# A four-layer graph network in which only the order lists of the five engines change

## The chip, the cores and the metric

The kernel runs on one core of one Trainium2 chip. The metric is device time in microseconds (us) from launch to end. Five engines work side by side, each through its own stream of instructions, in order: TensorE (PE, matmuls and transposes into PSUM), VectorE (DVE), ScalarE (ACT), GpSimd (POOL), and SyncE (SP), which here issues every DMA. They meet at semaphores only.

## The reference, cut to what matters

64 graphs of 256 nodes with 256 features pass through four layers. Each layer is `x = layernorm(x + layer(x))`, with one adjacency mask for all:

```python
# layer 0: e = leaky_relu((x W1)(x W2)^T), masked softmax, relu(att @ (x W3))
# layer 1: h = x W; e = leaky_relu(h a1 + (h a2)^T), masked softmax, elu(att @ h)
# layer 2: out = relu(x mlp1 + b1); unmasked graph attention (512 wide), elu, + residual;
#          relu(. mlp2 + b2); masked graph attention (256 wide), elu, + residual, relu
# layer 3: q, k, v = x wq^T + bq, ...; 4 heads of 64; masked softmax(q k^T / 8) @ v; @ wo^T + bo
```

The 64 graphs don't depend on one another. Matmuls of layers 0 to 2 and of the projections are made three times, on high and low parts of both operands (`hi*lo`, `lo*hi`, `hi*hi`).

## The kernel before, in words

One graph is one sample `t`. Everything of a sample is cut into steps, each on one engine: a few instructions with the semaphores that they wait for. The names say what a step belongs to. PE has `g0 h0 s0 t0 a0 x0` (layer 0: two products, scores, transposes of the probabilities, attention product, transposes of the normalised result), `h1 f1 t1 a1 x1` (layer 1), `m2 n2 c2 r2 f2 d2 b2 v2 w2` (layer 2, first part), `m3 n3 h3 f3 t3 a3 o3 x3` (second part), `q4 k4 v4 s40 s42 a4 y4` (layer 3). The same name on ACT, DVE or POOL is mostly the step that takes that product out of PSUM: ACT rounds to the high part, DVE (or POOL) computes the low part. On DVE `e0 e1 e3` mask the scores, `st`, `ag` take the moments of a layernorm, `n4` applies the last one; on POOL `v0 v1 v3 v4` make its factor, `n0 n1 n3` apply it, and `a0` adds the residual to layer 0's result.

The kernel is a software pipeline, and its order is written out in `ORDERS` (line 9 of kernel.py on): one string for each engine, in which `name:stage` means that in round `k` this engine runs this step for sample `k - stage`. `run` unrolls such a string over 64 samples plus the highest stage. Rounds have no barrier. What is set by a string is the sequence on one engine; rotating a string, with the stages raised by one behind the cut, gives the same sequence.

Layer 3's attention runs through DRAM. For heads 0 and 1 (half 0) and heads 2 and 3 (half 1) PE makes scores (`s40`, `s42`, line 436). DVE masks them (`s40` to `s43`, line 935). ACT takes the exponential (`p40` to `p43`, line 671), DVE a reciprocal (line 944), and POOL multiplies (`d4x`, `p4x`, lines 1060 and 1067). DVE transposes blocks of 32 (`x40`, `x42`, line 950). SP writes the half to DRAM (`o40`, `o42`, line 200, 512 KB) and, once that has landed, reads it back turned (`i40`, `i42`, line 208, four DMAs of 128 KB each). Then PE's `a4` (line 456) multiplies with v: eight matmuls of half 0, a wait, eight of half 1.

SP also loads the sample twice, turned (`lt`, line 186, into `x0T`, which waits until POOL's `l0` of the sample before has read it) and straight (`lx`, line 190, into `x0`, which waits for POOL's `a0` of the sample before), and stores the result (`st`, line 194). `x0T`, `x0` and `p4T` have one buffer each.

Banks 2 and 3 of PSUM are lent in turn to `x3 h3 x0 x1 o3 h1`: each of these PE steps (by `enter`) waits until the one before it has been read out; `h1` so waits for DVE's `r3` (line 898).

Of the kernel before, what the change touches and what calls it, by code (L numbers as in the profile page):

```python
# [5 lines left out]


ORDERS = {
    "sp": "lt:0 o40:7 st:9 o42:7 lx:1 i40:7 i42:7",
    "pe": "h3:8 a0:3 v4:9 f3:8 x0:5 g0:2 s40:9 d2:7 x1:6 t3:8 s42:9 v2:7 a3:8 m2:6 h0:2 b2:7 n2:6 o3:8 w2:7 s0:2 h1:5 c2:6 f1:5 t0:2 a4:9 r2:6 t1:5 x3:8 y4:9 m3:7 n3:7 a1:5 f2:6 q4:8 k4:8",  # L10
    "ac": "t0:3 r2:7 x3:9 m3:8 o3:8 a1:6 f2:7 q4:9 k4:9 h3:8 w2:7 x2:7 a0:3 u3:8 x0:5 p3:8 g0:2 p40:9 t3:8 x1:6 p41:9 p42:9 a3:8 p43:9 m2:6 b3:8 b2:7 h0:2 n2:6 o2:6 s0:2 h1:5 y2:7 p0:2 c2:6 k2:7 u1:5 a4:9 p1:5 z2:7 l0:1 t1:5",
    "dv": "e0:1 st3:7 h1:4 st0:2 n2:6 ag3:7 ag0:2 c2:5 i2:6 e1:4 j2:6 a4:8 z2:6 x3:7 i1:4 t1:4 i0:1 ag4:9 y4:8 r2:5 t0:1 f2:5 st4:8 b1:4 a1:4 b2:5 q4:7 st1:4 ag1:4 h3:6 k4:7 v4:7 e3:6 x0:3 s40:7 s41:7 g0:0 p40:7 t3:6 s42:7 x1:4 p41:7 i3:6 s43:7 p42:7 d2:5 n4:9 c3:6 p43:7 x40:7 b3:6 h0:0 x42:7 a3:6 r3:6 v2:5 z3:6",
    "po": "n1:5 d40:8 p40:8 d41:8 p41:8 d42:8 p42:8 d43:8 p43:8 m2:5 a0:2 v3:7 n3:7 v0:2 l0:0 k4:8 v4:9 m3:6 y1:4 n0:2 v1:4 w2:5",
}


# [1097 lines left out]
```

## Time and profile before

| what | value |
|---|---|
| median of 3 runs | 2921.05 us (2909.83 to 2933.94) |
| the profiled execution | 2918.28 us, its span 2916.5 us |
| PE busy | 2689.4 us, 92% of the span |
| DVE, ACT, POOL busy | 78%, 69%, 53% |
| DMA | 195.17 MB, mean 67 GB/s |
| mean granted TensorE clock | 0.983 |

The profiled execution lies 2.8 us under the median. Its span is counted from the first to the last instruction; 1.8 us lie around it. Busy shares are means over a fill of some 250 us, a long steady part and an end in which stages run out.

### The profile page before, as it was taken

Reading aid. Unit: us, or ns where it says so; the run is one execution under the profiler, and the core shown is the slowest. Engines: PE = TensorE matmul, PEld = TensorE weight load, DVE = VectorE, ACT = ScalarE, POOL = GpSimd, SP = SyncE. Lnnn points to the kernel's source line nnn. Section 1 sums busy time; section 2 is a strip of 40 time slices with the busy share of each in tenths; the row PEclk is TensorE's granted clock in tenths of the full one; section 3 lists DMA queues with packets and bytes.
Section 4 is the critical chain, followed back from the end, with each engine's and each line's share of the span. In section 5 each row is a group of like instructions: output and inputs, shape, how many; then the busy total and the mean of one; then the engine's idle time right before and its main releaser. Section 6 shows DMA issues by size and latency. Waiting matters only on the chain.

```text
span 2916.5 us, 61536 instructions
## 1 busy us (share of the span) xinstructions
PE 2689.4 (92%) x22472; PEld 2551.3 (87%) x22472; DVE 2278.2 (78%) x6124; ACT 1998.7 (69%) x4801; POOL 1556.0 (53%) x2119
## 2 busy tenths in 40 slices
PE   4689999999999999999999999999999999999974
PEld 4589999999999999998999998999999999998863
DVE  3257888888888888888888887888888888888874
ACT  1357777777777776777777777777777777776752
POOL 0235555555555555555556555555655555555542
PEclk9799999999999999999999999999999999999997
DMA  3001222222122122212212221221222122122222
GB/s 109 19 16 37 77 81 64 57 81 80 41 80 81 59 63 80 74 47 81 80 51 71 81 72 49 81 81 48 74 81 70 52 80 80 41 81 73 66 66 73
DMA packets 132766, 195.17 MB, mean 67 GB/s; under 512 B 14832, under 2 KB 97136, under 8 KB 132464
## 3 DMA queue, kind: packets, MB, share of 16 engines
q1 hardware_dynamic: 132464, 191.24, 22.7%
q8 instruction: 178, 2.92, 0.4%
q14 instruction: 124, 1.02, 0.1%
HBM read 107.30 MB, written 83.89 MB: 66 GB/s over the span
## 4 chain that ended last, share of the span: by engine, by line
PE 60%; DMA 13%; ACT 8%; SPq 8%; DVE 6%; issue 4%; POOL 1%; POOLq 0%; DVEq 0%
PE ps L224 29%; DMA p4T<-scratch 10%; PE ps L378 6%; SPq L208 6%; PE ps L240 5%; PE ps L436 4%; PE ps L337 4%; PE ps L233 3%; PE ps L338 3%; DMA scratch<-p 3%; DVE p L950 3%; PE ps L456 2%; ACT p L671 2%; PE ps L360 2%; DVE h_lo L692 1%
## 5 line engine op out<-in xcount | busy, mean ns | idle before, releaser
L1067 POOL TENSOR_TENSOR p<-p,rd 128x512 f32<-128x512 f32 x256 | 269.8, 1054 | 20.0
L671 ACT ACTIVATE p<-p,nmx 128x256 f32<-128x256 f32 x512 | 255.7, 504 | 25.4 <-DVE nmx L935 25.2
L991 POOL TENSOR_TENSOR o1Tp_lo<-o1T,o1Tp_hi 128x1024 fp32r<-128x1024 f32 x64 | 153.8, 2403 | 220.8 <-ACT o1Tp_hi L472 220.8
L1003 POOL TENSOR_SCALAR xn<-act,nmean,rstd 128x256 f32<-128x256 f32 x384 | 243.6, 643 | 18.3 <-POOL rstd L998 11.2
L456 PE MATMUL ps<-p4T,v 128*64 128x256 f32 x1024 | 144.3, 404 | 118.2 <-DMA p4T<-scratch 117.7
L995 POOL TENSOR_TENSOR vare<-mv,eps 128x2 f32<-128x2 f32 x256 | 108.0, 422 | 270.5 <-DVE mv L748 270.5
L1060 POOL TENSOR_TENSOR rd<-some,den 128x2 f32<-128x2 f32 x256 | 53.5, 209 | 354.6 <-DVE den L944 354.6
L456 PEld LDWEIGHTS ps<-p4T,v 128*64 128x64 f32 x1024 | 67.3, 140 | 178.1 <-DMA p4T<-scratch 96.5
L692 DVE TENSOR_TENSOR xnT_lo<-ps,xnT_hi 128x512 fp32r<-128x512 f32 x192 | 132.1, 688 | 114.2 <-ACT xnT_hi L472 114.2
L935 DVE CUSTOM_DVE_ANT_0 p<-ps,mask 128x256 f32<-128x256 f32 x512 | 189.9, 418 | 33.3 <-PE ps L436 33.3
L480 ACT ACTIVATE sco<-sco,nmax 128x256 f32<-128x256 f32 x384 | 191.0, 500 | 28.9 <-DVE nmax L736 28.9
L991 POOL TENSOR_TENSOR x0Tp_lo<-x0T,x0Tp_hi 128x512 fp32r<-128x512 f32 x64 | 112.7, 1761 | 162.4 <-ACT x0Tp_hi L472 162.4
L472 ACT ACTIVATE h_hi<-ps 128x512 fp32r<-128x512 f32 x192 | 114.7, 597 | 112.9 <-PE ps L233 98.6
L998 POOL TENSOR_TENSOR rstd<-vare,mhalf 128x2 f32<-128x2 f32 x256 | 179.7, 702 | 0.0
L736 DVE CUSTOM_DVE_ANT_0 sco<-ps,mask 128x256 f32<-128x256 f32 x384 | 146.4, 417 | 40.0 <-ACT ps L475 40.0
L475 ACT ACTIVATE ps<-ps,cols 128x256 f32<-128x256 f32 x384 | 154.5, 441 | 33.7 <-PE ps L246 33.1
L612 ACT ACTIVATE o3T<-ps,b2m 128x256 f32<-128x256 f32 x128 | 53.8, 471 | 171.3 <-PE ps L378 171.3
L337 PE MATMUL ps<-w_fc_lo,o1Tp_hi 128*128 128x258 f32 x512 | 154.8, 302 | 8.5 <-POOL o1Tp_lo L991 5.9
L692 DVE TENSOR_TENSOR h_lo<-ps,h_hi 128x512 fp32r<-128x512 f32 x192 | 131.1, 683 | 38.4 <-ACT h_hi L472 38.4
L742 DVE BATCH_NORM_STATS2 stat<-act 128x6 f32<-128x256 f32 x384 | 143.4, 414 | 19.9 <-POOL act L1013 14.6
L950 DVE STREAM_TRANSPOSE p<-p 128x1024 f32<-128x1024 f32 x128 | 157.4, 1230 | 0.7 <-POOL p L1067 0.7
L224 PE MATMUL ps<-pfcp_lo,hfc_hi 128*128 128x256 f32 x512 | 155.6, 304 | 2.1 <-ACT rdb L472 2.1
(248 smaller groups left out, 12683.1 us busy)
## 6 DMA issues: line engine op xcount, KB each, us to landing
scratch<-p SPq DMA_DIRECT2D x128, 512.0 KB, 2.9
p4T<-scratch SPq DMA_DIRECT2D x512, 128.0 KB, 3.9
x0T<-in_xT SPq DMA_DIRECT2D x64, 256.0 KB, 4.6
x<-in_x SPq DMA_DIRECT2D x64, 256.0 KB, 3.7
out<-xn SPq DMA_DIRECT2D x64, 256.0 KB, 3.0
o1T<-in_mlp SPq DMA_DIRECT2D x1, 512.0 KB, 4.4
p<-in_mlp SPq DMA_DIRECT2D x1, 512.0 KB, 4.5
att<-in_fc SPq DMA_DIRECT2D x1, 512.0 KB, 5.4
```

The costliest lines, as they stand in the source:

```text
L224: ins = nc.tensor.matmul(dst[:, m, :], lhs[a][:, k, (off + m) * P:(off + m + 1) * P], rhs[b][:, k, :], start=(k == 0 and i == 0), stop=(k ...
L337: nc.tensor.matmul(ps[:, 4, 0:C2], lhs, WP["fc"][b][:, k, 0:C2], start=(k == 0 and i == 0), stop=(k == HT - 1 and i == 2))
L456: ins = nc.tensor.matmul(bank[6][g * HD:(g + 1) * HD, c, :], v4[:, k, h * HD:(h + 1) * HD], p4Tv[:, c, g, k, :, :, :], start=(k == 0), sto ...
L480: ins = nc.scalar.activation(sco[i][:, m, :], sco[i][:, m, :], ACT.Exp, scale=-1.0, bias=nmax[i][:, m:m + 1], accum_out=den[i][:, m:m + 1])
L671: ins = nc.scalar.activation(rows_, rows_, ACT.Exp, scale=-1.0, bias=nmx4[:, h, m:m + 1], accum_out=den4[:, h, m:m + 1])
L692: return V.tensor_tensor(pair[1][:, :, :], whole, pair[0][:, :, :].bitcast(fp32), ALU.subtract)
L935: ins = V.tensor_tensor_reduce(p4v[h // 2][:, h % 2, m, :, :, :].rearrange("p w b j -> p w (b j)"), bank[7 - h % 2][:, m, :].rearrange("p ...
L950: V.transpose(p4[c][:, :, :], p4[c][:, :, :]).then_inc(S["p4x"], 1)
L991: return G.tensor_tensor(lo, whole, hi.bitcast(fp32), ALU.subtract)
L998: G.tensor_tensor(rstd[i][:, :], vare[i][:, :], mhalf[:, :], ALU.pow).then_inc(s_rs, 1)
L1003: ins = G.tensor_scalar(xn[:, m, :], y[:, m, :], nmean[i][:, m:m + 1], rstd[i][:, m:m + 1], ALU.add, ALU.mult)
L1067: G.tensor_tensor(rows_, rows_, rd4[:, h, :].unsqueeze(2).unsqueeze(3).broadcast_to([P, NT, QUADS, CT * QP]), ALU.mult).then_inc(S["p4n"], 1)
```

## The change

Every engine's string is another one. No step, instruction, wait or buffer differs; what differs is the sequence in which each engine comes to them.

```diff
-    "sp": "lt:0 o40:7 st:9 o42:7 lx:1 i40:7 i42:7",
-    "pe": "h3:8 a0:3 v4:9 f3:8 x0:5 g0:2 s40:9 d2:7 x1:6 t3:8 s42:9 v2:7 a3:8 m2:6 h0:2 b2:7 n2:6 o3:8 w2:7 s0:2 h1:5 c2:6 f1:5 t0:2 a4:9 r2:6 t1:5 x3:8 y4:9 m3:7 n3:7 a1:5 f2:6 q4:8 k4:8",
-    "ac": "t0:3 r2:7 x3:9 m3:8 o3:8 a1:6 f2:7 q4:9 k4:9 h3:8 w2:7 x2:7 a0:3 u3:8 x0:5 p3:8 g0:2 p40:9 t3:8 x1:6 p41:9 p42:9 a3:8 p43:9 m2:6 b3:8 b2:7 h0:2 n2:6 o2:6 s0:2 h1:5 y2:7 p0:2 c2:6 k2:7 u1:5 a4:9 p1:5 z2:7 l0:1 t1:5",
-    "dv": "e0:1 st3:7 h1:4 st0:2 n2:6 ag3:7 ag0:2 c2:5 i2:6 e1:4 j2:6 a4:8 z2:6 x3:7 i1:4 t1:4 i0:1 ag4:9 y4:8 r2:5 t0:1 f2:5 st4:8 b1:4 a1:4 b2:5 q4:7 st1:4 ag1:4 h3:6 k4:7 v4:7 e3:6 x0:3 s40:7 s41:7 g0:0 p40:7 t3:6 s42:7 x1:4 p41:7 i3:6 s43:7 p42:7 d2:5 n4:9 c3:6 p43:7 x40:7 b3:6 h0:0 x42:7 a3:6 r3:6 v2:5 z3:6",
-    "po": "n1:5 d40:8 p40:8 d41:8 p41:8 d42:8 p42:8 d43:8 p43:8 m2:5 a0:2 v3:7 n3:7 v0:2 l0:0 k4:8 v4:9 m3:6 y1:4 n0:2 v1:4 w2:5",
+    "sp": "lt:0 i40:8 lx:1 i42:8 o40:7 st:9 o42:7",
+    "pe": "c2:6 f1:5 x3:8 a4:9 r2:6 t1:5 m3:7 n3:7 y4:9 a1:5 f2:6 q4:8 t0:2 h3:7 k4:8 v4:8 f3:7 a0:2 x0:4 s40:8 g0:1 t3:7 s42:8 x1:5 d2:6 a3:7 m2:5 o3:7 b2:6 h0:1 n2:5 v2:6 w2:6 h1:4 s0:1",
+    "ac": "m3:8 o3:8 a1:6 f2:7 q4:9 t0:3 h3:8 w2:7 k4:9 u3:8 x2:7 a0:3 p3:8 x0:5 p40:9 t3:8 p41:9 x1:6 g0:2 p42:9 p43:9 a3:8 m2:6 b2:7 b3:8 h0:2 n2:6 o2:6 y2:7 h1:5 k2:7 c2:6 u1:5 z2:7 s0:2 a4:9 p1:5 x3:8 r2:6 t1:5 p0:2 l0:1",
+    "dv": "r3:7 z3:7 v2:6 st3:7 ag3:7 n2:6 h1:4 i2:6 j2:6 c2:5 e1:4 z2:6 n4:9 st0:2 ag0:2 a4:8 e0:1 x3:7 t1:4 r2:5 y4:8 i1:4 i0:1 f2:5 b1:4 st4:8 a1:4 b2:5 q4:7 t0:1 h3:6 st1:4 ag1:4 k4:7 v4:7 e3:6 s40:7 s41:7 x0:3 p40:7 i3:6 t3:6 s42:7 p41:7 x1:4 s43:7 p42:7 ag4:8 g0:0 d2:5 p43:7 x40:7 c3:6 x42:7 b3:6 h0:0 a3:6",
+    "po": "n0:3 v1:5 n1:5 w2:6 d40:8 p40:8 d41:8 p41:8 d42:8 p42:8 d43:8 p43:8 v4:9 a0:2 m2:5 v3:7 n3:7 v0:2 m3:6 l0:0 y1:4 k4:7",
```

Rotated to one starting point, the strings differ by local moves; the stages change only as the cut goes. On PE, `x1` and `d2` go behind `s42`, `x3` ahead of `a4`, `t0` from ahead of `a4` to behind `q4`, `y4` behind `n3`, `k4` behind `h3`, `a0` behind `f3`, `g0` behind `s40`, and the end of the round is `o3 b2 h0 n2 v2 w2 h1 s0` in place of `h0 b2 n2 o3 w2 s0 h1`. On SP the sequence from `x40` on was `o40 st o42 lx i40 i42 lt`; it becomes `o40 st o42 lt i40 lx i42`, with `lx` for one sample later. On DVE, `n4` leaves its place ahead of `x40`, `b3` and `h0` go behind `x42`, `ag4` comes ahead of `g0`, and `z3` ahead of `v2`. On POOL `v4` and `a0` come directly behind `p43`, ahead of `m2`, `l0` behind `m3`, `n1` ahead of `w2`, and `k4` to the end of the round behind `y1`. On ACT `p43` goes ahead of `a3`, `s0` behind `z2`, `p0` and `l0` to the end behind `t1`, `t0` behind `q4`.

## Rows read from the trace of the kernel before

**Rows 1.** Busy time by engine in the steady part (windows; TensorE's clock, DMA share, GB/s last)

```profile
265.00:2530.00 2265.00, 2182.31 (x18594) 2083.74 (x18593) 1863.76 (x5041) 1653.37 (x3979) 1296.41 (x1751) 1.00 0.24 69
```

**Rows 2.** Waits of PE (total, times, longest): steady part, then its whole span

```profile
PE ps L456 <- DMA p4T<-scratch: 82.3, 82, 1.8
...
PE ps L456 <- DMA p4T<-scratch: 117.7, 92, 12.4
```

**Rows 3.** Timeline of SP: loads of x0T, 55 rounds apart (start, duration)

```profile
256.61 0.43 SPq L186 DMA_DIRECT2D x0T<-in_xT  x1
...
2601.20 0.43 SPq L186 DMA_DIRECT2D x0T<-in_xT  x1
```

**Rows 4.** Timeline of PE around one a4

```profile
1452.72 0.60 PE L240 MATMUL ps<-ident,sco 128*128 128x128 f32 x4
1453.25 1.08 PE L456 MATMUL ps<-p4T,v 128*64 128x256 f32 x8
1455.27 1.08 PE L456 MATMUL ps<-p4T,v 128*64 128x256 f32 x8 [0.93 <-DMA p4T<-scratch]
```

**Rows 5.** Chain of waits, one round, from d2 and s42 to a4's second half

```profile
1434.61 0.98 PE ps L360 x8
...
1436.55 0.91 PE ps L436 x12
...
1445.21 1.16 DVE p L950
...
1450.97 4.26 DMA p4T<-scratch
```

**Rows 6.** Timeline of DVE in the same round: n4, c3, x40, b3, h0, x42, z3

```profile
1440.06 1.07 DVE L972 TENSOR_SCALAR xn<-xn,nmean,rstd 128x256 f32<-128x256 f32 x2
1441.41 0.90 DVE L885 TENSOR_SCALAR act<-act 128x512 f32<-128x512 f32 x1 [0.28 <-ACT act L640]
...
1442.47 1.23 DVE L950 STREAM_TRANSPOSE p<-p 128x1024 f32<-128x1024 f32 x1
1443.73 0.50 DVE L889 TENSOR_SCALAR act<-act 128x512 f32<-128x512 f32 x1
1444.52 0.69 DVE L692 TENSOR_TENSOR h_lo<-ps,h_hi 128x512 fp32r<-128x512 f32 x1 [0.29 <-ACT h_hi L472]
1445.13 1.23 DVE L950 STREAM_TRANSPOSE p<-p 128x1024 f32<-128x1024 f32 x1
...
1448.96 1.04 DVE L902 SCALAR_TENSOR_TENSOR act<-act,xn 128x512 f32<-128x512 f32 x1
```

**Rows 7.** Chain of waits near the end, where SP has no loads left

```profile
2832.22 3.36 DMA scratch<-p
...
2836.89 3.37 DMA p4T<-scratch
```

**Rows 8.** A window of 1 us in the burst of transfers of rows 5

```profile
1454.00:1455.00 1.00, 0.33 (x4) 0.00 (x0) 1.00 (x2) 1.00 (x3) 0.82 (x2) 1.00 1.02 213
```

**Rows 9.** Timeline of PE: first product after transposes

```profile
1418.11 0.37 PE L224 MATMUL ps<-w_woT_lo,qT_hi 128*128 128x256 f32 x1
1418.31 0.28 PE L224 MATMUL ps<-w_woT_hi,qT_lo 128*128 128x256 f32 x1
1418.43 0.28 PE L224 MATMUL ps<-w_woT_hi,qT_hi 128*128 128x256 f32 x1
```

**Rows 10.** One line's instructions, 1000 to 2000 us: ns min/median/max

```profile
L902 DVE SCALAR_TENSOR_TENSOR act<-act,xn x23: 1045/1052/1067, 1020.9 to 1959.9; 128x512 f32<-128x512 f32 x23
...
L806 DVE TENSOR_SCALAR act<-act x23: 408/412/413, 1039.7 to 1979.3; 128x512 f32<-128x512 f32 x23
```

**Rows 11.** Timeline of POOL in the same round: p43, m2, a0

```profile
1442.91 1.04 POOL L1067 TENSOR_TENSOR p<-p,rd 128x512 f32<-128x512 f32 x1
1447.06 2.40 POOL L991 TENSOR_TENSOR o1Tp_lo<-o1T,o1Tp_hi 128x1024 fp32r<-128x1024 f32 x1 [3.11 <-ACT o1Tp_hi L472]
1450.35 1.31 POOL L1013 TENSOR_TENSOR act<-act,x 128x512 f32<-128x512 f32 x1 [0.89 <-DMA x<-in_x]
```

## The prediction, written before the changed kernel was run

> **What bounds the kernel now.** I read the windows first. In the steady part PE is busy for 2182.3 of 2265 us, at full granted clock; DVE has 82%, ACT 73%, POOL 57% [rows 1]. So PE is the bound, and 82.7 us of it are idle. The list of PE's waits for the same stretch has one line: 82.3 us for the landing of `p4T`, in `a4` [rows 2]. The reader is to see that this is the only loss of PE there. The round lasts (2601.20 - 256.61) / 55 = 42.63 us [rows 3], the stretch holds 53.1 of them, and the idle time is 1.55 us a round. The timeline shows where: eight matmuls of half 0 from 1453.25, half 1 only at 1455.27 [rows 4]. Matmuls start 0.12 us apart [rows 9], so half 1 could have started at 1454.21; it is 1.06 us late where the profile calls 0.93 idle. By that ratio the 1.55 us are worth some 1.75 us of round. The round without the wait would be 40.9 us.
>
> The chain of waits says what ends it. PE's `s42` ends at 1437.46, DVE's transpose `x42` at 1446.37, half 1 lands at 1455.23 [rows 5]: 8.9 us over ACT, POOL and DVE, then 8.9 us of transfers. In these the DMA engines are full (share 1.02 at 213 GB/s in the last window but one) [rows 8], so the landing is a matter of bytes queued ahead, not of latency alone.
>
> **The change part by part.** All terms are per round of the profiled execution, 2918.3 us, whose span is 1.8 us less; it lies 2.8 us under the median of the runs, 0.1%, which I neglect.
>
> PE's cover. Between `s42` and `a4` PE gains `x1`, `d2` and `x3` and loses `t0`. Four transposes in a row are 0.53 us to the next step (1452.72 to 1453.25) [rows 4], `d2` is 0.98 [rows 5]. Net +0.53 + 0.98 + 0.53 - 0.53 = 1.5 us; as neighbouring transposes are a little cheaper I take 1.4 (1.2 to 1.5).
>
> The chain from `s42` to `x42`. `n4`, 1.07 us, stood on DVE ahead of `c3` and `x40`; it goes to a place 25 us off. `b3` and `h0` stood between the end of `x40` (1443.70) and `x42` (1445.13), 1.43 us with their waits [rows 6]; they go behind. What is late next: `x42` needs POOL's `p43`, which in this round ends at 1443.95 [rows 11], 1.2 us ahead of `x42`'s start. It comes earlier too, since `p43` on ACT no longer stands behind `a3`, which waits for PE. `ag4` is added ahead of `x40` (0.2, two small aggregates). `c3` now waits for an `a3` on ACT that stands behind `p43`. Bounds: 0.8 (only the slack before `x42` is won) to 2.3 (all of 1.07 + 1.43 - 0.2). I take 1.4, as ACT and POOL keep some of it.
>
> The transfers. Before, `x0` (256 KB) was ahead of half 0, `x0T` (256 KB) behind half 1. Afterwards both are ahead of the last of half 1. In this round `x42`'s end to landing is 8.86 us. It is a quick one: its waits are 0.93 where the mean is 1.55, so the mean is some 9.5. Near the end, where SP has no loads, the same stretch is 2832.22 to 2840.26 = 8.04 us [rows 7]. So the two loads cost 1.5 us together, one ahead and one behind. With both ahead I take +0.5 (0 if the one behind already cost as much, 1.2 if it is one more whole load at 213 GB/s). SP's own queue is no limit: `lt` and `lx` are two issues of 0.43 us [rows 3], and half 1's issues are done some 4.3 us before the landing [rows 5].
>
> The Trainium skill says in DMA: Bandwidth & Descriptors, Queues, rings and completion order, that one issuing engine's descriptors are consumed in ring order on each DMA engine. By that rule a load issued ahead delays half 1 by its whole transfer and one issued behind by nothing. The sum would take the upper end, 1.2. The trace disagrees in part, since two loads with one ahead cost 1.5.
>
> Sum of the chain: late by 1.75 before, cover +1.4, chain -1.4, transfers +0.5: half 1 lands 0.55 us before PE wants it. Single waits ran up to 1.8 us against a mean of 1.0 each [rows 2], so some rounds still wait: 0.1 a round.
>
> `lx` between `i40` and `i42` waits for POOL's `a0` of the sample before, so a late `a0` would hold half 1. In this round `a0` ran from 1450.35 to 1451.66, behind `m2` [rows 11], which would hold `i42` by over 3 us. But `a0` now comes directly behind `p43` and `v4` (some 1.0 us): it ends 2.3 us after `p43`. SP comes to `lx` at least the transpose (1.2), `o42`, `lt` and four issues (2.7) after `p43`, 3.9 us: no wait, with 1.6 us to spare. `lt` waits for `l0`, which POOL's string still has half a round ahead. The store between `o40` and `o42` no longer waits for an `n4` of the same moment; nothing is won there.
>
> Switches of PE. The first product after transposes takes 0.20 us to the next instead of 0.12 [rows 9]. The old sequence has seven groups of transposes that a product follows (`f1 t0`, `t1 x3`, `f2`, `f3 x0`, `x1 t3`, `b2`, `o3`), the new one nine (`f1 x3`, `t1`, `f2`, `t0`, `f3`, `x0`, `t3`, `x1`, `o3 b2`): 2 x 0.08 = +0.16.
>
> POOL beside DVE. `z3` took 1045 to 1067 ns in all 23 rounds, though `b1`, as many elements, took 408 to 413 [rows 10]; each time it began while POOL's `m2` ran (1447.06 to 1449.46) and ended 0.5 us after it, at 1450.0 [rows 6, 11]. `c3` took 0.90 beside the 0.50 of `b3` [rows 6]. So some DVE operations don't run beside a POOL operation. Now `z3` comes right behind `r3`, near the start of `m2` (2.40 us), and `a0` (1.31) comes to lie over `b3`. Behind `b3` stand `a3` and `r3`, for which PE's `h1` waits; behind `z3` stand `v2`, `st3`, `ag3`, POOL's `n3` and so PE's `x3`, which now comes ahead of `a4`: from `x42`'s end 10.5 us (9.5 + 0.5 + 0.55) until half 1 is wanted, less 0.96 and 0.53, is 9.0, against some 8 us of these DVE and POOL steps; 1 us of slack. Bounds 0 and 2.2 us a round; I take +0.3, since half a wait of 1.31 at `b3` is met by the 1.07 us that `n4` gave back.
>
> The other steps keep covers of some tenths (`v4` to `s40`, `s41` to `s42`, `a0` to `g0`, `m2` to `n2`), about as wide as before, where no wait is listed; nothing for them. Fill: layer 0's steps keep their sequence among themselves; 0, give or take 5.
>
> Sum: -1.75 + 0.1 + 0.16 + 0.3 = -1.2 us a round. For the 57 samples whose `a4` lies ahead of SP's last load that is -68. The last seven rounds hold 117.7 - 82.3 = 35 us of waits with the first of fill and end [rows 2], where the shorter chain gives back some 5. 2918.3 - 73 = 2845 us, 2.5% less.
>
> **The rivals.** First, all of it is won: no new wait at all. For it speaks the only line in rows 2; -1.75 + 0.16 = -1.6 a round, with 8 at the end: 2819 us. Second, half is eaten: either collisions of POOL and DVE cost 1 us a round, or the loads cost their 1.2 and the chain gives 0.8 (1.75 - 1.4 - 0.8 + 1.2 leaves 0.75 of wait). Then -0.6 to -0.7 a round: 2880 us. Third, the change doesn't do what it says: another loop stands right behind and PE waits elsewhere for as long; 2910 us. Against it speaks that in 53 rounds nothing but `a4` ever waited.
>
> Fourth, slower, by one mechanism: DVE and POOL block each other at `b3` and `z3`. If `z3` comes just after `m2` has begun, it waits the whole 2.40 us rather than 0.5, so 1.9 more, and `b3` up to 1.3 for `a0`; less the 1 us of slack at `x3` that is 2.2 us on PE. With 0.16 that is 2.4 against 1.75: +0.6 a round, 2952 us. It decides from 1.6 us of new waits a round on. The Trainium skill, SBUF — State Buffer, Who interferes with whom, states this rule: VectorE with two SBUF inputs and GpSimd reading SBUF exclude each other for a whole instruction, and whoever starts first blocks the other. By that rule the trace agrees at `z3`, and a moved step may pay more or less than it did.
>
> **How the numbers follow.** Forecast 0.50 (own range 2828 to 2865), all won 0.15, half eaten 0.17, no gain 0.09, slower 0.09. Under 1%, or 29 us, this kernel's measurement can't tell a change from none. Faster by over 1% (below 2892) are the forecast, all won, and most of half eaten: 0.77; within 1% 0.14; slower 0.09. For 8 in 10 the range leaves out the slower case and the outer tails of the rest: 2812 to 2905.
>
> **What would show it.** In the new trace: the line of `a4`'s waits down from 1.55 to 0.1 a round and the round at 41.4 us (right); half 1 landing 9.5 to 10.5 us after `x42`'s end; `s42` to `x42` 7.5 us rather than 8.9. New lines among PE's waits with L233 (for L898) or L240 (for `n3`) would show the port; a wait on L456 still over 0.5 would show the transfers. Wrong altogether it would be by a wait that sits in none of these loops.

## The result, and the profile after

| what | before | after |
|---|---|---|
| median | 2924.36 us (4 runs, 2909.83 to 2933.94) | 3016.74 us (4 runs, 3011.54 to 3023.52) |
| ratio, 95% interval | | 1.0319 (1.0281 to 1.0357) |
| profiled execution, its span | 2918.28, 2916.5 us | 3017.15, 3015.4 us |
| mean granted TensorE clock | 0.983 | 0.970 |
| round in the steady part | 42.63 us | 44.41 us |

The change made the kernel 3.2% slower, where 2.5% faster was forecast. A round is read from one execution of a kernel; those of the kernel before spread over 24 us in this batch, 0.4 us a round, so a difference of a few tenths between rounds counts only where the medians bear it out. The windows of the changed kernel over its steady part (columns as in [rows 1]), then the waits of PE there, then one line of the same list for the whole span:

```profile
300.00:2600.00 2300.00, 2167.77 (x18156) 2047.36 (x18156) 1921.65 (x4922) 1605.74 (x3890) 1269.93 (x1709) 0.99 0.24 66
```

```profile
PE ps L240 <- POOL xn L1003: 108.3, 51, 2.1
PE ps L337 <- DVE att L846: 23.9, 52, 0.5
...
PE ps L456 <- DMA p4T<-scratch: 12.4, 1, 12.4
```

Set these beside [rows 1, 2]. The wait for the transfers is gone: 82.3 us became nothing in the steady part, and one wait in the fill. Two others took its place, each in every round: `x3` waits 108.3 / 51 = 2.12 us for POOL's `n3`, and `c2` waits 0.46 us for DVE's `v2` (line 846). So 1.55 us of idle time a round went and 2.58 came. The clock of 0.99 is the third loss.

The timeline of SP gives the round, (2592.51 - 283.16) / 52 = 44.41 us, and the new sequence of transfers, with `lx` between the two halves and no pause at it (the last lines are one round):

```profile
283.16 0.42 SPq L186 DMA_DIRECT2D x0T<-in_xT  x1
...
1394.07 0.44 SPq L186 DMA_DIRECT2D x0T<-in_xT  x1
1394.61 2.37 SPq L208 DMA_DIRECT2D p4T<-scratch  x4
1397.02 0.43 SPq L190 DMA_DIRECT2D x<-in_x  x1
1397.55 1.80 SPq L208 DMA_DIRECT2D p4T<-scratch  x4
...
2592.51 0.45 SPq L186 DMA_DIRECT2D x0T<-in_xT  x1
```

The timeline of PE in the same round answers to [rows 4]: the first product of `c2`, the transposes of `f1`, then `x3` and `a4`. The last two lines are the same two steps one round later.

```profile
1400.81 0.36 PE L337 MATMUL ps<-w_fc_lo,o1Tp_hi 128*128 128x258 f32 x1 [0.47 <-DVE att L846]
...
1403.76 0.38 PE L246 MATMUL ps<-ident,cols 128*128 128x128 f32 x2
1406.27 1.11 PE L240 MATMUL ps<-ident,xn 128*128 128x128 f32 x4 [2.13 <-POOL xn L1003]
1407.31 3.02 PE L456 MATMUL ps<-p4T,v 128*64 128x256 f32 x16
...
1451.65 0.66 PE L240 MATMUL ps<-ident,xn 128*128 128x128 f32 x4 [2.14 <-POOL xn L1003]
1452.24 1.95 PE L456 MATMUL ps<-p4T,v 128*64 128x256 f32 x16
```

`a4` is one piece of sixteen matmuls now: both halves had landed long before. The same `x3` and `a4` took 2.54 us (1451.65 to 1454.19) in one round and 4.06 us in the other. The windows over four successive `x3` show why (the clock stands third from the end):

```profile
1405.80:1409.20 3.40, 2.94 (x14) 1.85 (x16) 3.40 (x11) 1.54 (x2) 0.41 (x1) 0.54 0.00 0
1450.00:1453.40 3.40, 1.75 (x16) 1.22 (x18) 3.40 (x8) 2.17 (x4) 1.60 (x2) 1.00 0.02 5
1494.50:1497.90 3.40, 2.40 (x20) 1.48 (x20) 3.40 (x10) 1.56 (x3) 0.95 (x1) 1.00 0.00 0
1539.00:1542.40 3.40, 3.05 (x14) 1.95 (x16) 3.40 (x10) 1.45 (x2) 0.30 (x1) 0.53 0.00 0
```

In every third round, right after the wait, the granted clock is at the 1.2 GHz level (0.54 and 0.53 with the edges of the window), otherwise at 2.4. The trace has 17 such stretches from 300 to 2600 us, 58.0 us together; before it had one, of 3.4 us. At 1.5 us lost in every third round that is an estimated 0.5 us a round.

Why `n3` is late stands in the timelines of DVE and POOL [rows 6, 11 show before]. DVE from `x42` to `j2`, then POOL:

```profile
1392.44 1.23 DVE L950 STREAM_TRANSPOSE p<-p 128x1024 f32<-128x1024 f32 x1
1393.60 1.32 DVE L889 TENSOR_SCALAR act<-act 128x512 f32<-128x512 f32 x1
...
1397.13 2.40 DVE L902 SCALAR_TENSOR_TENSOR act<-act,xn 128x512 f32<-128x512 f32 x1
1399.45 1.21 DVE L846 TENSOR_TENSOR att<-ps,rdb 128x1024 f32<-128x1024 f32 x1
...
1401.79 0.69 DVE L851 TENSOR_SCALAR ex<-ex 128x1024 f32<-128x1024 f32 x1 [0.18 <-ACT ex L597]
...
1403.07 1.21 DVE L855 SCALAR_TENSOR_TENSOR att<-att,o1T 128x1024 f32<-128x1024 f32 x1
1404.39 1.39 DVE L860 TENSOR_TENSOR att<-ex,att 128x1024 f32<-128x1024 f32 x1
```

```profile
1393.35 1.29 POOL L1013 TENSOR_TENSOR act<-act,x 128x512 f32<-128x512 f32 x1
1396.59 2.39 POOL L991 TENSOR_TENSOR o1Tp_lo<-o1T,o1Tp_hi 128x1024 fp32r<-128x1024 f32 x1 [1.96 <-ACT o1Tp_hi L472]
...
1401.85 0.68 POOL L996 TENSOR_SCALAR nmean<-mv 128x2 f32<-128x2 f32 x1
...
1403.38 2.83 POOL L1003 TENSOR_SCALAR xn<-act,nmean,rstd 128x256 f32<-128x256 f32 x2 [0.18 <-POOL rstd L998]
```

Read the pairs that overlap. `b3` (L889) ends at 1394.92, 0.3 us after `a0` (L1013). `z3` (L902) began 0.54 us after `m2` (L991) and ends 0.55 us after it; the chain of waits has 2.07 of its 2.40 us as "issue", time in which the profile shows nothing waited for. Then it goes the other way: POOL's `n3`, two operations that take 0.55 us each when alone, is under way while DVE does `i2` and `j2` (L855, L860). Its first operation ends at 1404.71, 0.43 us after `i2`, its second 0.43 us after `j2`: each is held by one of the two. L996 of `v3` takes 0.68 us beside L851 where 0.19 is usual. Means over 44 samples of either trace, before and after: `b3` 0.50 and 1.32, `z3` 1.04 and 2.40, `v3` 1.02 and 1.51, `n3` 1.60 and 2.83 us.

The same stretch of the kernel before, DVE and then POOL, shows that `n3` already ran beside `i2`, and not beside `j2` as well:

```profile
1454.13 1.21 DVE L855 SCALAR_TENSOR_TENSOR att<-att,o1T 128x1024 f32<-128x1024 f32 x1
1455.26 0.41 DVE L736 CUSTOM_DVE_ANT_0 sco<-ps,mask 128x256 f32<-128x256 f32 x1
...
1455.95 1.43 DVE L860 TENSOR_TENSOR att<-ex,att 128x1024 f32<-128x1024 f32 x1
```

```profile
1454.70 1.60 POOL L1003 TENSOR_SCALAR xn<-act,nmean,rstd 128x256 f32<-128x256 f32 x2 [0.18 <-POOL rstd L998]
```

Between `i2` and `j2` stood `e1` (L736), in which `n3`'s second operation ran at its 0.55 us. The new DVE string has `e1` behind `j2`. The list of moves ahead of the prediction doesn't name this one, nor `c3` going behind `x40`, nor ACT's and DVE's `p41` going ahead of `x1`; all three are in the strings themselves.

### The profile page after: what moved, and what is told of

Read it like the earlier page. It is cut to its first block, busy times and chain, and to the rows that moved or that the text cites. A ratio compares the mean times of both kernels' runs of the same rounds, so it can differ in the third digit from the quotient of the medians.

```text
span 3015.4 us, 61536 instructions
## 1 busy us (share of the span) xinstructions
PE 2731.7 (91%) x22472; PEld 2567.3 (85%) x22472; DVE 2381.5 (79%) x6124; ACT 1989.0 (66%) x4801; POOL 1569.1 (52%) x2119
## 3 DMA queue, kind: packets, MB, share of 16 engines
q14 instruction: 124, 1.02, 0.1%
## 4 chain that ended last, share of the span: by engine, by line
PE 54%; DVE 19%; POOL 9%; ACT 9%; issue 7%; SPq 0%; DMA 0%; POOLq 0%; DVEq 0%; ACTq 0%
PE ps L224 24%; PE ps L378 6%; POOL xn L1003 6%; ACT p L671 6%; PE ps L240 5%; PE ps L456 5%; DVE p L950 5%; PE ps L337 4%; PE ps L233 3%; PE ps L338 3%; DVE att L846 3%; DVE act L889 2%; PE ps L436 2%; DVE act L801 2%; POOL rstd L998 1%
## 5 line engine op out<-in xcount | busy, mean ns | idle before, releaser
L1003 POOL TENSOR_SCALAR xn<-act,nmean,rstd 128x256 f32<-128x256 f32 x384 | 316.7, 833 | 23.2 <-POOL rstd L998 22.3
L991 POOL TENSOR_TENSOR o3Tp_lo<-o3T,o3Tp_hi 128x512 fp32r<-128x512 f32 x64 | 82.5, 1290 | 417.4 <-ACT o3Tp_hi L472 417.4
L995 POOL TENSOR_TENSOR vare<-mv,eps 128x2 f32<-128x2 f32 x256 | 61.3, 240 | 445.7 <-DVE mv L748 445.7
L240 PE MATMUL ps<-ident,xn 128*128 128x128 f32 x768 | 131.9, 298 | 146.4 <-POOL xn L1003 146.3
L597 ACT ACTIVATE ex<-att 128x1024 f32<-128x1024 f32 x64 | 67.9, 1060 | 255.9 <-DVE att L846 255.9
L240 PEld LDWEIGHTS ps<-ident,xn 128*128 128x128 f32 x768 | 89.5, 148 | 170.4 <-POOL xn L1003 161.7
L991 POOL TENSOR_TENSOR o1Tp_lo<-o1T,o1Tp_hi 128x1024 fp32r<-128x1024 f32 x64 | 154.3, 2412 | 148.3 <-ACT o1Tp_hi L472 148.3
L337 PE MATMUL ps<-w_fc_lo,o1Tp_hi 128*128 128x258 f32 x512 | 156.7, 306 | 33.8 <-DVE att L846 27.4
L961 DVE TENSOR_TENSOR xn<-ps,xb 128x512 f32<-128x512 f32 x64 | 44.3, 692 | 143.1 <-PE ps L224 143.1
L337 PEld LDWEIGHTS ps<-w_fc_lo,o1Tp_hi 128*128 128x128 f32 x512 | 97.5, 190 | 69.3 <-issue 61.7
L736 DVE CUSTOM_DVE_ANT_0 sco<-ps,mask 128x256 f32<-128x256 f32 x384 | 145.6, 416 | 10.4 <-ACT ps L475 9.6
L378 PE MATMUL ps<-o2T_lo,w_mlp_hi 128*128 128x256 f32 x512 | 149.0, 291 | 0.0
L224 PE MATMUL ps<-xnT_lo,w_mlp_hi 128*128 128x256 f32 x512 | 144.6, 282 | 4.4 <-ACT o1T L561 2.4
```

Of the source, the lines that this page charges most:

```text
L224: ins = nc.tensor.matmul(dst[:, m, :], lhs[a][:, k, (off + m) * P:(off + m + 1) * P], rhs[b][:, k, :], start=(k == 0 and i == 0), stop=(k ...
L240: ins = nc.tensor.transpose(dst[:, b, a * P:(a + 1) * P], src[:, a, b * P:(b + 1) * P], ident[:, :])
L337: nc.tensor.matmul(ps[:, 4, 0:C2], lhs, WP["fc"][b][:, k, 0:C2], start=(k == 0 and i == 0), stop=(k == HT - 1 and i == 2))
L378: ins = nc.tensor.matmul(bank[3][:, m, :], WP["mlp2"][a][:, k, m * P:(m + 1) * P], o2T[b][:, k, :], start=(k == 0 and i == 0), stop=(k == ...
L991: return G.tensor_tensor(lo, whole, hi.bitcast(fp32), ALU.subtract)
L1003: ins = G.tensor_scalar(xn[:, m, :], y[:, m, :], nmean[i][:, m:m + 1], rstd[i][:, m:m + 1], ALU.add, ALU.mult)
```

## The experiments

The theory after the result: the transfers did what was forecast, and the loss is in DVE and POOL operations that hold each other up on the way from `x42` to `n3`, which PE now wants before `a4`. Rivals: `x3` and `c2` would be late without that; or the transfers' new sequence costs in some hidden way. Medians are given with the ratio to the kernel before in the same batch; waits are PE's, 300 to 2500 us, total, times, longest.

**`x3` alone goes back (PE).**

```diff
-c2:6 f1:5 x3:8 a4:9 r2:6 t1:5 m3:7
+c2:6 f1:5 a4:9 r2:6 t1:5 x3:8 m3:7
```

> The changed kernel with x3 alone put back on PE, behind t1. In the changed kernel x3 waits 2.1 us a round for n3, and the granted clock falls to half for 3.41 us after every third such wait. If x3's place is what turns POOL's late n3 into a loss of PE, both go: the round falls from 44.4 to 41.3 us (40.9 of PE's work and 0.45 of c2's wait for v2), the run to 2840 us, and no stretch at half clock is left between 300 and 2600 us. If the loop over DVE and POOL (x42, b3, a3, r3, z3, v2, st3, n3) is the bound by its own length, the wait moves to another PE step behind x3 and the round stays above 43.5 us, the run above 2970 us.

Measured: 2874.27 us, 0.9882 (0.9856 to 0.9907), round 42.11, no stretch at the low clock.

```profile
PE ps L337 <- DVE hfc_lo L826: 24.9, 51, 0.5
PE ps L337 <- DVE att L846: 23.8, 52, 0.5
```

With one move undone the round is 2.30 us shorter, more than the waits it removed (2.12, with 0.49 new), as the clock came back too. It stays above the 2840 expected: `c2` still waits for `v2`, and `r2`, which comes earlier without the pause, waits for the low part of `c2`'s result. Both stand on DVE behind `z3`, still 2.39 us long. The expectation had left this second wait out.

**`z3` alone goes back behind `v2` (DVE).**

```diff
-r3:7 z3:7 v2:6 st3:7
+r3:7 v2:6 z3:7 st3:7
```

> The changed kernel with z3 alone put back behind v2 on DVE. Theory of the shared port: z3 starts 1.1 us later and still ends when POOL's m2 lets go, so its duration falls from 2.40 to some 1.3 us while its end, and with it st3, v3 and the start of n3, stay; v2 ends 2.3 us earlier and c2's wait of 0.46 us for it goes; i2 and j2 move 2 us ahead, so n3 is held by j2 alone and shrinks from 2.83 to about 2 us: round 43.0 to 43.6 us, run 2930 to 2965 us. If instead z3 lasts 2.40 us for a reason of its own, it stays at 2.4 us, ends 1.1 us later, and the run is slower than 3017 us.

Measured: 2917.38 us, 1.0022 (1.0007 to 1.0037), round 42.57, no low clock. `z3` is down to 0.96 and `c2` no longer waits, but `x3` does:

```profile
PE ps L240 <- POOL xn L1003: 77.2, 51, 1.6
```

It came out lower than expected: the clock's loss went as well, in this run with 1.5 us of waits a round, where the changed kernel had 2.1 + 0.5. One thing of the expectation was wrong: `n3` was to be held by `j2` alone and to fall to 2 us; it takes 2.67, and is beside both still.

**The rule itself: shorten one partner.** POOL's `m2` computes 2 of 256 columns; the rest of the low part is set to zero once ahead of the loop.

```diff
-low_part(o1Tp[1][:, :, :], o1T[t % 2][:, :, :], o1Tp[0][:, :, :]).then_inc(S["o1Tl"], 1)
+low_part(o1Tp[1][:, :, 0:2], o1T[t % 2][:, :, 0:2], o1Tp[0][:, :, 0:2]).then_inc(S["o1Tl"], 1)
```

> The changed kernel in which POOL's m2 computes 2 of 256 columns of the low part of the hidden layer (the rest stays zero), all orders as they are: it leaves that work out and nothing else. Theory of the shared port: with no long POOL operation beside it, DVE's z3 falls from 2.40 to 0.55 us in the same place; v2 and st3 end 1.8 us earlier. b3 stays at 1.32 us (held by a0) and n3 at over 2 us. The wait for n3 falls from 2.1 to under 1 us, round 42 to 42.6 us. If z3's 2.40 us has another cause than m2, it stays.

Next, DVE's `i2` and `j2` on 2 of 256 columns, which leaves the residual of layer 2's first half out of the rest:

```diff
-V.scalar_tensor_tensor(att[:, :, :], att[:, :, :], 0.0, o1T[t % 2][:, :, :], ALU.max, ALU.add).then_inc(S["res"], 1)
+V.scalar_tensor_tensor(att[:, :, 0:2], att[:, :, 0:2], 0.0, o1T[t % 2][:, :, 0:2], ALU.max, ALU.add).then_inc(S["res"], 1)
...
-V.tensor_tensor(att[:, :, :], ex2[:, :, :], att[:, :, :], ALU.add).then_inc(S["o2"], 1)
+V.tensor_tensor(att[:, :, 0:2], ex2[:, :, 0:2], att[:, :, 0:2], ALU.add).then_inc(S["o2"], 1)
```

> The changed kernel in which DVE's i2 and j2 work on 2 of 256 columns (the residual of layer 2's first half is left out for the rest), all orders as they are. Theory of the shared port: POOL's v3 and n3, two small steps of 0.55 us each in n3, are held by i2 and j2, operations with two SBUF inputs; so n3 falls from 2.83 to some 1.1 us, v3 from 1.51 to 1.0 us, x3's wait goes from 2.1 to under 0.3 us, and the round falls to 41.5 to 42.3 us, while z3 stays at 2.40 us beside m2. If n3 is late only because z3 is, n3 keeps its 2.83 us and the wait stays above 1.5 us.

Measured, one execution each and so without an interval: 2896.06 us (round 42.19) and 2873.11 us (round 42.12). Line 902 from 1000 to 2000 us (ns min/median/max), first in the changed kernel, then with `z3` back, then with the small `m2`, and with small `i2` and `j2` last:

```profile
L902 DVE SCALAR_TENSOR_TENSOR act<-act,xn x23: 2386/2402/2412, 997.7 to 1975.0; 128x512 f32<-128x512 f32 x23
```

```profile
L902 DVE SCALAR_TENSOR_TENSOR act<-act,xn x24: 957/962/969, 1004.8 to 1983.9; 128x512 f32<-128x512 f32 x24
```

```profile
L902 DVE SCALAR_TENSOR_TENSOR act<-act,xn x24: 691/691/693, 1001.6 to 1971.9; 128x512 f32<-128x512 f32 x24
```

```profile
L902 DVE SCALAR_TENSOR_TENSOR act<-act,xn x23: 2386/2399/2410, 1032.7 to 1959.3; 128x512 f32<-128x512 f32 x23
...
L1003 POOL TENSOR_SCALAR xn<-act,nmean,rstd x142: 548/554/572, 1015.3 to 1986.9; 128x256 f32<-128x256 f32 x142
```

`z3`, untouched in both, falls to 0.69 us when `m2` is short, and stays at 2.40 when it isn't; `n3` (L1003), untouched, falls from 2.83 to 1.09 us for its two operations when `i2` and `j2` are short. That settles who holds whom. `v3` stayed at 1.51, which the expectation had at 1.0: not these two, and by the overlap its partner is L851, which no run shortened. The waits are 57.2 us in 52 (`x3`) with the small `m2`, 1.1 each where under 1 was expected, and 23.6 in 52 (`c2`) and 20.2 in 52 (`x3`) with the other, 0.39 at `x3` where under 0.3 was.

**Both moves go back.** The first and the second diff together.

> The changed kernel with both moves undone at once: x3 behind t1 on PE, z3 behind v2 on DVE. With x3 alone put back 0.46 us a round were left in which c2 waits for v2, and 0.47 in which r2 waits for c2's low part, both behind z3's 2.40 us. Theory of the shared port: z3 behind v2 frees v2 and what follows by 1 to 2 us, so both go: round 41.1 to 41.3 us, run 2815 to 2835 us. If z3 is not what held v2, the run stays at 2870 us.

Measured: 2815.05 us, 0.9673 (0.9651 to 0.9694), round 41.09.

```profile
PE ps L456 <- DMA p4T<-scratch: 7.2, 12, 1.3
```

So all other moves together are worth 3.3%, and two moves turn that into 3.2% lost. Each makes the other dearer: against this kernel the round is 1.48 us longer with `x3` moved alone (42.57), 1.02 longer with `z3` moved alone (42.11), and 3.32 with both, where the two add up to 2.50. An estimated 0.5 of the difference is the clock, which falls only with both.

**Single gains put into the kernel before.** First the cover: `g0`, `x1`, `d2` on PE, and `g0` on ACT and DVE.

```diff
-pe: x0:5 g0:2 s40:9 d2:7 x1:6 t3:8 s42:9 v2:7
+pe: x0:5 s40:9 g0:2 t3:8 s42:9 x1:6 d2:7 v2:7
-ac: p3:8 g0:2 p40:9 t3:8 x1:6 p41:9
+ac: p3:8 p40:9 t3:8 x1:6 g0:2 p41:9
-dv: s41:7 g0:0 p40:7 t3:6 s42:7 x1:4 p41:7 i3:6 s43:7 p42:7 d2:5
+dv: s41:7 p40:7 t3:6 s42:7 x1:4 p41:7 i3:6 s43:7 p42:7 g0:0 d2:5
```

> The kernel before with one part of the change alone: x1 and d2 behind s42 on PE (and g0 behind s40, with ACT's and DVE's g0 moved along), which puts 1.4 us more of PE's work between s42 and a4. DVE, POOL and SP keep their old places otherwise. If the cover acts as the sum had it, a4's wait falls from 1.8 us (start to start) to 0.4 to 0.6 a round, nothing else waits, and the run is 2835 to 2855 us. If the new waits of the changed kernel come from the PE order as such, others appear, as large.

Then the chain, DVE's `b3` and `h0` behind `x42`:

```diff
-x40:7 b3:6 h0:0 x42:7
+x40:7 x42:7 b3:6 h0:0
```

> The kernel before with another part alone: on DVE b3 and h0 behind x42 in place of ahead of it. x42 then starts when POOL's p43 ends, 1.2 us earlier. If the chain acts as the sum had it, s42 to x42 falls from 8.9 to 7.7 us, a4's wait from 1.8 to 0.6 us a round, and the run is 2845 to 2860 us. If the transfers were the bound and the transpose were not, half 1 would land when it did and the time would stay at 2911 us.

And both:

> Both parts of the last two kernels together on the kernel before. x3 and z3 keep their old places, a0 stays behind m2, SP's string is the old one, so that the collisions of the changed kernel (a0 with b3, m2 with z3, i2 and j2 with n3) don't arise. Theory: 2.6 us of lead against a wait of 1.8, so PE waits nowhere: round 40.9 to 41.1 us, run 2805 to 2825 us, faster than both kernels. If a loop over DVE or POOL stands right behind the one removed, the gain is less than the sum of the two single ones.

| kernel | median, ratio | round | `s42` to `x42` | `x42` to landing | wait on `p4T` |
|---|---|---|---|---|---|
| before | | 42.63 | 8.90 | 9.55 | 80.7, 80, 1.8 |
| cover | 2943.16, 1.0119 (1.0100 to 1.0138) | 42.91 | 10.18 | 9.43 | 75.2, 74, 2.0 |
| chain | 2880.19, 0.9899 (0.9877 to 0.9920) | 42.04 | 7.77 | 10.10 | 53.8, 67, 1.5 |
| both | 2914.06, 1.0018 (1.0004 to 1.0032) | 42.46 | 9.10 | 10.13 | 55.7, 67, 1.6 |

(Means over 44 samples.) The cover alone is a loss, and the expectation had it as a gain. Its timeline of ACT shows why:

```profile
1312.71 0.49 ACT L671 ACTIVATE p<-p,nmx 128x256 f32<-128x256 f32 x1
...
1313.20 0.58 ACT L472 ACTIVATE o3Tp_hi<-ps 128x512 fp32r<-128x512 f32 x1
1314.51 0.60 ACT L472 ACTIVATE xnT_hi<-ps 128x512 fp32r<-128x512 f32 x1 [0.74 <-PE ps L240]
1315.01 0.59 ACT L472 ACTIVATE gT_hi<-ps 128x512 fp32r<-128x512 f32 x1
1315.48 0.51 ACT L671 ACTIVATE p<-p,nmx 128x256 f32<-128x256 f32 x1
```

ACT takes `x1` and `g0` out of PSUM between `p40` and `p41`. With `x1` behind `s42` on PE, ACT waits 0.74 us for it, and `p41` stands behind; the softmax chain that the cover was to hide grows by 1.3 us. The chain alone gave 1.1 us at `x42`, as expected, but the transfers took back 0.55 of it, so the run stays above the 2845 to 2860 expected. Both together were to leave no wait and take 2805 to 2825; they are no faster than before. `s42` to landing is 0.78 us longer than before, so that of a cover of 1.4 only 0.6 counts, and the cover brings a wait of its own, of `s40` for DVE's low part of v, since `g0` no longer stands ahead of `s40`:

```profile
PE ps L436 <- DVE v L928: 11.2, 51, 0.2
```

That is 0.22 us a round, in all four runs that put this cover into the kernel before. What else the cover costs these runs stays open: with it alone the waits have grown by 0.1 us a round and the round by 0.28.

**The cover with its ACT sequence.** `p41` ahead of `x1` on ACT and DVE, `p43` ahead of `a3` on ACT; then the same with `b3`, `h0` behind `x42`.

```diff
-ac: t3:8 x1:6 g0:2 p41:9 p42:9 a3:8 p43:9
+ac: t3:8 p41:9 x1:6 g0:2 p42:9 p43:9 a3:8
-dv: s42:7 x1:4 p41:7 i3:6
+dv: s42:7 p41:7 x1:4 i3:6
```

> The kernel before with the PE cover (g0, x1, d2 moved) as in the run that came out slower, and with ACT's p41 ahead of x1, p43 ahead of a3 and DVE's p41 ahead of x1, as the changed kernel has them. There s42 to x42 grew from 8.90 to 10.18 us because ACT's p41 stood behind x1, which now waits for a later PE step. Theory: with ACT's order mended s42 to x42 is 8.4 to 8.9 us, the cover of 1.4 us counts in full, a4's wait falls to 0.1 to 0.5 us and the run is 2825 to 2855 us. If the cover as such lengthens the chain, s42 to x42 stays over 10 us and the run at 2940 us.

> The kernel before with all the coupled moves between s42 and a4 at once, and no others: PE's g0, x1 and d2; ACT's g0, p41 ahead of x1, p43 ahead of a3; DVE's p41 ahead of x1, g0 behind p42, b3 and h0 behind x42. x3, z3, a0, n4 and SP stay. In the last run x42 still stood behind b3 and h0, which wait for PE steps that the cover makes later. Theory: s42 to x42 falls from 10.18 to 7.4 to 8.0 us, landing 10.0 us after x42, a4's wait from 1.8 us (start to start) to under 0.3: round 41.0 to 41.3 us, run 2815 to 2840 us. If a cover of PE's work can't be had without lengthening the chain as much, s42 to x42 stays above 9 us and the run above 2880 us.

Measured: 2929.28 us, 1.0074 (1.0051 to 1.0098), `s42` to `x42` still 10.18, wait 67.8, 66, 1.8; and 2875.63 us, 0.9879 (0.9852 to 0.9906), `s42` to `x42` 8.42, wait 27.4, 41, 1.3. DVE of the first:

```profile
1308.01 1.29 DVE L972 TENSOR_SCALAR xn<-xn,nmean,rstd 128x256 f32<-128x256 f32 x2
...
1311.70 0.43 DVE L889 TENSOR_SCALAR act<-act 128x512 f32<-128x512 f32 x1 [0.40 <-ACT act L645]
1312.76 0.69 DVE L692 TENSOR_TENSOR h_lo<-ps,h_hi 128x512 fp32r<-128x512 f32 x1 [0.63 <-ACT h_hi L472]
1313.37 1.24 DVE L950 STREAM_TRANSPOSE p<-p 128x1024 f32<-128x1024 f32 x1
```

What ACT wins, DVE gives back: `b3` and `h0`, ahead of `x42`, now wait 0.40 and 0.63 us for ACT. Without them it takes 8.42, not the 7.4 to 8.0 expected, and neither run reaches the time expected (2825 to 2855, then 2815 to 2840). `n4` (L972, 1.29), which the full change moves away, may be the largest piece of what then lies between 8.42 and 6.98; it was not moved by itself. The landing took back a part here too, 10.20 after 9.27.

**The transfers.** The new string of SP in the kernel before; the old one in the kernel with `x3` and `z3` back; the old one in the changed kernel with POOL's `a0` behind `m2`; and, last, both loads behind half 1, with `x3` and `z3` back.

```diff
-lt:0 o40:7 st:9 o42:7 lx:1 i40:7 i42:7
+lt:0 i40:8 lx:1 i42:8 o40:7 st:9 o42:7
```

> The kernel before with the changed SP string alone (lt ahead of i40, lx between i40 and i42, one sample later). lx now waits for POOL's a0, which here still stands behind m2 and ends at 45.1 us of the round, while SP comes to it at 42.4: i42 is held some 2 us, and half 1 has one more load ahead of it (the changed kernel's landing is 10.6 us after x42's end, before it was 9.55). Theory: x42's end to landing 11.5 to 12 us, a4's wait 1.8 + 1.5 to 2.3 us a round, run 2990 to 3050 us. If the order of SP's issues is only a matter of bytes ahead, the landing comes at 10.6 us and the run is 2970 us.

> The kernel with x3 and z3 put back, and SP's string of before with it. That kernel still waits 7 us in all for p4T between 300 and 2500 us, with half 1 landing 10.67 us after x42's end. With one load behind half 1 it should land at 9.5 to 9.7 us; the 12 waits left go: run 5 us less, 2808 to 2812 us, which the interval can hardly tell from none. If the extra microsecond of landing is due to the transpose coming earlier and not to the load ahead, it stays at 10.6 us.

```diff
-sp: lt:0 i40:8 lx:1 i42:8 o40:7 st:9 o42:7
+sp: lt:0 o40:7 st:9 o42:7 lx:1 i40:7 i42:7
-po: v4:9 a0:2 m2:5 v3:7
+po: v4:9 m2:5 a0:2 v3:7
```

> The changed kernel with POOL's a0 put back behind m2, and SP's old string so that a0 has its data. Theory of a string of collisions: b3 is not held by a0 any more (1.32 to 0.5 us), r3 ends 0.9 us earlier, z3 starts just ahead of m2 instead of just behind it and falls from 2.40 to 0.6 us; v2 and st3 end 2.7 us earlier, but v3 stands behind a0, which ends 1 us after them. x3's wait falls from 2.1 to 0.3 to 1.0 us a round, no stretch at half clock is left, run 2860 to 2905 us. If a0 over b3 doesn't matter, z3 keeps 2.40 us and the run stays above 2970 us.

```diff
-sp: lt:0 i40:8 lx:1 i42:8 o40:7 st:9 o42:7
+sp: i40:8 i42:8 lt:0 lx:1 o40:7 st:9 o42:7
```

> The best kernel so far (the changed one with x3 and z3 put back) with both loads behind half 1 on SP: i40 i42 lt lx o40 st o42, lx still one sample ahead, so that a0 behind p43 has its data. Half 1 then has no load ahead of it. Theory of bytes ahead: x42's end to landing falls from 10.67 to between 8.1 (as at the end of the kernel before, without loads) and 9.5 us; the 7 us of waits for p4T between 300 and 2500 us go, the round falls from 41.09 to 40.95 us, run 2803 to 2812 us, 0.965 of before. If the landing is a matter of the burst as a whole (all transfers of the round together), it stays at 10 us or more and the time doesn't move.

| kernel | median, ratio | round | landing | loads ahead of half 1 |
|---|---|---|---|---|
| new SP alone | 3033.68, 1.0443 (1.0403 to 1.0483) | 44.67 | 10.40 | both |
| both back, old SP | 3009.19, 1.0353 (1.0326 to 1.0380) | 44.50 | 9.70 | one |
| `a0` back, old SP | 2913.31, 1.0024 (1.0007 to 1.0041) | 42.59 | 9.69 | one |
| both back (above) | 2815.05, 0.9673 | 41.09 | 10.67 | both |
| both back, loads last | 2803.21, 0.9641 (0.9617 to 0.9665) | 40.83 | 8.70 | none |

The first three kernels: PE's largest wait in each, with SP's for the first and POOL's for the second behind it:

```profile
PE ps L456 <- DMA p4T<-scratch: 120.3, 65, 3.6
...
SPq L190 <- POOL act L1013: 79.5, 49, 1.7
```

```profile
PE ps L337 <- POOL o1Tp_lo L991: 116.5, 49, 5.3
...
POOL act L1013 <- DMA x<-in_x: 248.2, 49, 7.5
```

```profile
PE ps L240 <- POOL xn L1003: 81.6, 51, 3.9
```

The new string alone is the slowest kernel of all. Its `lx` waits 79.5 / 49 = 1.6 us for an `a0` that comes behind `m2`, with `i42` queued behind: what the prediction found to be covered by `a0`'s new place is not covered without it. Yet half 1 lands only 0.85 us later than before, less than expected. The rest of the 2.04 us a round is the clock: 143 us at the low level from 300 to 2600 us, if half of them are lost, is an estimated 1.4 a round. The other way round it is as bad. With the old string `lx` is issued only just ahead of `i40`, for the `a0` of the same moment, and `a0`, which the change put ahead of `m2`, waits 248.2 / 49 = 5.1 us for it with `m2` behind; the expectation had overlooked this. With `a0` back behind `m2`, `b3` is down to 0.38 and `z3` to 0.69, and yet `x3` waits 1.6 us, where 0.3 to 1.0 was expected: `a0` (1.29) now stands between `m2` and `v3`, `v3` starts as it ends, and `n3` still takes 2.65. In these two runs `a0` costs one path or the other while `x3` comes ahead of `a4`.

The last kernel is 3.6% faster than before. From the one with both loads ahead it isn't clearly apart in time, as their intervals overlap; its landing is. PE has no idle time in its steady part:

```profile
300.00:2500.00 2200.00, 2200.00 (x18861) 2110.44 (x18860) 1929.37 (x5122) 1656.77 (x4041) 1305.41 (x1781) 1.00 0.24 72
```

Half 1 is there 1.93 us before PE wants it, where it was 0.19 with both loads ahead.

## Why the prediction was wrong, point by point

**The bound, and the wait to be removed: right.** The loss was all in `a4`; without it and without a new one the round is 40.83 us, against the 40.9 worked out.

**The cover, +1.4: right.** Before, PE wanted half 1 at 8.90 + 9.55 + 0.04 - 1.75 = 16.7 us after `s42`; with both moves back 6.98 + 10.67 + 0.19 - 0.13 (its mean wait) = 17.7, and `x3`'s 0.53 would make that 18.2: +1.5. That cover needs its ACT moves too was not in the term; the change had them.

**The chain, -1.4: too small.** 8.90 became 6.98, so -1.9, inside the bounds of 0.8 and 2.3.

**The transfers, +0.5: too small.** 9.55 became 10.62, +1.07, near the upper end of 1.2. One load ahead costs 0.85 to 1.0 us where little else differs: 8.70, 9.70 and 10.67 with none, one and two in the kernel with both moves back, 9.55 and 10.40 in the kernel before. The rest goes by the transposes: all with one load ahead, half 1 lands 9.27 us after `x42` where `x42` ends 3.3 us after `x40`, 9.43 and 9.55 at 2.6 and 2.7, 9.70 at 1.9, and 10.10 to 10.20 at 1.5. So of the +1.07 an estimated 0.9 is the load and 0.15 the closer halves, for which the sum had no term. I had read the trace as speaking against ring order, because two loads cost 1.5 with only one ahead; but the 8.04 it rested on was a single reading near the end. The Trainium skill, DMA: Bandwidth & Descriptors, Queues, rings and completion order, has it that each DMA engine consumes an issuing engine's descriptors in ring order; the runs agree for loads ahead. The 0.66 between 8.70 and 8.04, with two loads behind and with none, remains open.

**`lx` and `a0`: right** for this kernel: SP goes from `i40` to `lx` to `i42` without a pause.

**The sum of the chain: right.** Its errors nearly cancel, 1.75 - 1.4 - 1.9 + 1.07 = -0.5, against the -0.55 forecast; the changed kernel has 3.9 us to spare only because PE comes later. That it comes out is partly luck, as two terms were off by 0.5 in opposite directions.

**Switches, +0.16: not seen.** With PE always busy the round is 40.83, 1.80 under before. Either the wait was worth 1.96 or the switches cost less; a difference of 0.16 can't be told from the spread of single executions.

**The ends, -5: not so.** The span less 55 rounds is 571.9 before, and 3015.4 - 55 x 44.41 = 572.9 after. With both moves back it is 548.6, 23 us less than before, which was not looked into.

**POOL beside DVE, +0.3: this is the step that failed.** The mechanism was named, as the fourth rival, with its place and sign; it was sized at 0.3 a round in the forecast, and at 2.2 at most. Four things went into the size:

- `z3`. The text had the two cases, 0.5 us of `m2` left or the whole of it, and gave no reason for taking neither. The order had one: before, `v2` (1.21 us) stood between `r3` and `z3`, and `z3` began 1.90 us after `m2` [rows 6, 11]. Take `v2` away and it begins 0.7 us after `m2` at the latest; the rows shown already gave the whole block. It was 0.54, in every round. +1.36.
- `b3` under `a0`: +0.82, named as a bound of 1.31.
- What the estimate of 8 us for the steps up to `n3` took over unchanged: `v3` and `n3` had 1.02 and 1.60 us, but those are times beside what DVE did then. Now L851 lies beside `v3`, which takes 1.51, and `j2` follows `i2` without `e1` between, so that `n3`'s second operation is held as well as its first: 2.83. +0.49 and +1.23. `n3` took 1.60 in the kernel before and in all six kernels built on it, and 2.65 to 2.84 in the changed one and in six of the seven built on it with `i2` and `j2` whole (2.16 with both moves back and the old SP string); `e1` was not moved by itself. The prediction only asked what POOL does to DVE, never what DVE does to POOL.
- `v2`, behind `z3`, has a reader of its own: `c2` waits 0.46 us. "Behind `z3` stand `v2`" was written down and PE's `c2` not looked up.

Together 0.82 + 1.36 + 0.49 + 1.23 = 3.9 us. The path from `x42` to the end of `n3` takes 1406.21 - 1393.67 = 12.5 us where 8 was estimated and 9.0 was allowed; the "1 us of slack" at `x3` was gone four times over. PE came to `x3` 10.5 us after `x42` (1404.14), 10.0 without its pause at `c2`; 12.5 less 10.0 is the 2.5 us of new idle time.

**The clock: not foreseen at all.** +0.5 a round.

The account of the round: -1.55 of idle time, +2.12 and +0.46, +0.5 for the clock makes +1.5, of 1.78 measured. The rest is of the size by which an idle time is smaller than the delay that it stands for: in [rows 4] 0.93 for 1.06, and 1.03 more idle time by that ratio is 1.2, so +1.7. The fourth rival's 2952 us had +0.6 a round.

The Trainium skill, SBUF — State Buffer, Who interferes with whom, was named in the prediction for the block at `z3`. It holds for either side: VectorE with two SBUF inputs and GpSimd reading SBUF exclude each other, and the first to start holds the other for its whole instruction. The runs with a small partner agree, 2.40 to 0.69 us for `z3` and 2.83 to 1.09 for `n3`. By that page the question was not how much `z3` had paid before but which of two neighbours starts first after the move.

## What to carry to other kernels

When a step is moved on DVE or POOL, its duration moves with it: list for each step on the new critical path what the other of the two engines runs at that time, in both directions, and price it by the whole instruction unless the order says who is first. A consumer moved forward on the bounding engine spends the slack of its producers; look up every reader of the producer and of all that is queued behind it. The orders of five engines are one choice: here the cover without its ACT and DVE sequence, or a load's place without its reader's, each turned a gain into a loss, so single moves are tried in the company of those that they need.

## What the runs showed of the hardware

The granted clock fell to the 1.2 GHz level for one stretch of 3.4 us in every third round, where PE had sat idle for 0.47 us ahead of `c2` and 2.13 ahead of `x3` in all of them. In ten of the experiments, whose single waits were at most 1.8 us, it never fell between 300 and 2600 us; in the kernel before it fell once, right behind two waits of 1.4 and 0.5 us; in the cover alone twice, behind waits of 1.0 and 0.8 and behind one of 1.8; with `a0` back twice, beside waits of 3.7 and 3.9; in the new SP string alone and the old one with both moves back it fell 37 times, 143 and 147 us together. By the estimates above it made up 0.5 of the 1.8 us here and, in the new SP string alone, 1.4 of 2.0.

A POOL operation with one input is held by a DVE operation with two: `n3`'s two, 0.55 us each alone, took 1.33 and 1.51, the first ending 0.43 us after `i2`, the second 0.43 us after `j2`. Each operation paid for one partner, and POOL's first got in between the two of DVE; before the change it ended 0.43 us after `i2` too. And `b3`, a DVE operation with one input, is held by POOL's `a0`: 0.38 us with `a0` elsewhere, 1.32 beside it.
